# Scores of a gated cross-attention block: one product of 127 rows a head, with the mask among its rows

## What is computed

```python
scores = einsum('bhqd,bhkd->bhqk', qh, kh) / sqrt(16)        # 16 heads of 16; q = layernorm(x), k = v = ctx
causal = triu(ones((256, 77)), k=1)                          # later keys
merged = where(causal == 1, causal, mask[:, None, None, :])  # and padded keys
attn = softmax(where(merged == 1, -inf, scores))
x = x + tanh(g_xattn) * (einsum('bhqk,bhkd->bhqd', attn, vh) @ W.T + b)
x = x + tanh(g_ffn) * ffn(layernorm(x))    # SwiGLU shared expert, two groups of four experts, the best two
```

## Time and profile before

| | us |
|---|---|
| median of 3 runs | 1140.37 |
| lowest and highest | 1137.81, 1147.08 |
| the profiled execution | 1138.31 |
| its span in the trace | 1136.6 |

### The profile page before, as it was taken

The page is one execution under the profiler, slowest core; times in us unless marked ns, Lnnn a source line. Parts: engine busy times, 40 slices in busy tenths (PEclk is TensorE's granted clock), DMA queues, the critical chain, the costliest instruction groups (busy, mean ns, idle before and its releaser), DMA issues.

```text
span 1136.6 us, 22381 instructions
## 1 busy us (share of the span) xinstructions
PE 1084.2 (95%) x7411; PEld 908.4 (80%) x7411; DVE 818.2 (72%) x1810; ACT 472.3 (42%) x722; POOL 520.0 (46%) x644
## 2 busy tenths in 40 slices
PE   5689999999999999999999999999999999999997
PEld 3467888888788787788888777888887888888886
DVE  7757786886876876877878676557544688888886
ACT  4565556555555555655555432233221111111111
POOL 5334447457357456465563534000001566666564
PEclk8989999999999999999999999999999899999999
DMA  8975748666765764766666112687652554555451
GB/s 157 244 159 120 147 102 129 135 126 102 146 137 123 119 146 106 113 141 128 99 128 145 29 55 74 209 260 242 214 173 104 163 157 154 163 166 150 148 175 64
DMA packets 106162, 160.64 MB, mean 141 GB/s; under 512 B 28828, under 2 KB 70718, under 8 KB 106048
## 3 DMA queue, kind: packets, MB, share of 16 engines
q1 hardware_dynamic: 94276, 121.18, 46.8%
q0 software_dynamic: 11776, 38.03, 11.1%
HBM read 75.24 MB, written 52.10 MB: 112 GB/s over the span
## 4 chain that ended last, share of the span: by engine, by line
PE 71%; issue 11%; DVE 7%; POOL 6%; DMA 3%; ACT 2%; SPq 1%; POOLq 0%; DVEq 0%; ACTq 0%
PE ps L764 16%; PE ps L811 12%; PE ps L709 7%; PE ps L726 7%; PE ps L813 6%; PE ps L631 4%; PE ps L796 3%; PE ps L619 3%; PE ps L662 2%; POOL tab_dram L1471 2%; PE ps L585 2%; PE ps L589 2%; POOL x L1447 2%; DMA regr<-regr 2%; PE ps L640 1%
## 5 line engine op out<-in xcount | busy, mean ns | idle before, releaser
L811 PE MATMUL ps<-regr,gh 128*128 x600 | 221.6, 407 | 0.2 <-issue 0.2
L888 ACT ACTIVATE Pt<-ps,pbias 77x1024 f32<-77x1024 f32 x128 | 141.6, 1106 | 98.2 <-PE ps L619 96.8
L813 PE MATMUL ps<-regr,gl 128*128 x600 | 170.0, 283 | 0.0
L811 PEld LDWEIGHTS ps<-regr,gh 128*128 128x128 f32 x600 | 113.8, 190 | 23.9 <-issue 0.6
L978 ACT ACTIVATE gh<-ps 128x512 fp32r<-128x512 f32 x75 | 44.8, 599 | 204.9 <-PE ps L796 204.9
L1189 DVE TENSOR_REDUCE mneg<-ps 128x8 f32<-128x616 f32 x128 | 100.4, 792 | 21.3 <-PE ps L589 21.1
L813 PEld LDWEIGHTS ps<-regr,gl 128*128 128x128 f32 x600 | 114.0, 190 | 0.0
L709 PE MATMUL ps<-x2h,winh 128*128 128x512 f32 x256 | 108.2, 423 | 0.6 <-DVE OHR L1093 0.6
L1379 POOL TENSOR_TENSOR gl<-gf,gh 128x512 fp32r<-128x512 f32 x64 | 82.7, 1293 | 42.8 <-ACT gh L850 42.6
L1447 POOL TENSOR_TENSOR x<-x,regf 128x512 f32<-128x512 f32 x32 | 41.1, 1285 | 132.7 <-DMA x<-in_x 132.7
L709 PE MATMUL ps<-x2h,winl 128*128 128x512 f32 x256 | 100.6, 393 | 0.0
(11 more groups left out here) (201 smaller groups left out, 2652.9 us busy)
## 6 DMA issues: line engine op xcount, KB each, us to landing
regr<-regr SPq DMA_DIRECT2D x96, 256.0 KB, 5.9
y_dram<-Pt SPq DMA_DIRECT2D x64, 256.0 KB, 2.4
regf<-in_x SPq DMA_DIRECT2D x32, 256.0 KB, 4.3
x<-in_x SPq DMA_DIRECT2D x32, 256.0 KB, 7.2
y_dram<-res SPq DMA_DIRECT2D x32, 256.0 KB, 2.4
regr<-regr SPq DMA_DIRECT2D x96, 77.0 KB, 6.9
x_dram<-x2h SPq DMA_DIRECT2D x14, 512.0 KB, 3.0
x_dram<-x2l SPq DMA_DIRECT2D x14, 512.0 KB, 3.8
```

The lines of the kernel that those rows point to most:

```text
L811: e.matmul(o, gh2[:, k % 3, fc, :], w2v[:, bass.ds(val, 1), fc, :, :].rearrange("p o h d -> p (o h) d"), start=fc == 0, stop=False, skip_g ...
L813: m = e.matmul(o[:, 0, :], gl2[:, k % 3, fc, :], w2v[:, bass.ds(val, 1), fc, 0, :].rearrange("p o d -> p (o d)"), start=False, stop=fc == ...
L888: e.activation(Pt[0:K, 4 * k:4 * k + 4, :].rearrange("k (n j) t -> k n (j t)", n=2), bank_of["sc", b, k][0:K, :, :], ACT.Exp, bias=pbias[: ...
```

## The change

1. The mask of later keys becomes part of the score product. `Kst` and `Xs` get 77 rows ahead of the others: `cauT` (now the transposed triangle, -3e38) for all heads in `Kst`, an identity for tokens 0 to 76 and zero behind in `Xs`. Both are written once (`own` on ACT, `diagonal` on DVE). The L614 products go. The rows are 77 (mask) + 3 x 16 (high, low, high of the keys) + 2 (maxima) = 127, still with 77 output rows and 256 columns.
2. The rows of the other head half are no longer zero: `Xs` is kept per half j as well, so each product sees its own 48 rows only. A query copy is cut in two, with 64 source rows into 16 rows: six DMAs of 128 KB for three of 256 KB. `maxT` writes 2 rows instead of 4.
3. The keys are sent for each batch row by itself: stage `spread` in slot 9 of every step, six DMAs with rows of 616 bytes. `Kst` has buffers for two batch rows where it had them for two pairs. `kv` moves from slot 11 of odd steps to slot 2 of the even step behind it, and waits for all key copies before it; `keys` moves to slots 4 and 6.
4. Padded keys are overwritten in `kf` by the first unpadded one (`ramp` falls from 77, and padded keys get 1000 less), which leaves the maximum as it is without a mask: stages `marks`, `table` and `pick` on DVE (three operations for two batch rows, slot 9 of odd steps), with a small table in DRAM from which `load_kv` also loads `pk` for the two rows. `pad`, `first`, the two long mask copies and POOL's L1440 go; of the L589 products those for t = 0 stay, with `caus` alone.

```diff
-    order += [("load_x", 0, 0), ("load_kv", 0, 0), ("load_x", 1, 0), ("consts", 0, 0), ("moments", 0, 0), ("kv", 0, 0),
-              ("masks", 0, 0), ("pads", 0, 0)]
+    order += [("load_x", 0, 0), ("load_masks", 0, 0), ("load_kv", 0, 0), ("load_x", 1, 0), ("consts", 0, 0), ("moments", 0, 0),
+              ("marks", 0, 0), ("pick", 0, 0), ("kv", 0, 0)]
...
-        put(i, ((1, "keys", 0), (3, "keys", 1)))
+        put(i, ((1, "keys", 0), (3, "keys", 1)) if i == 0 else ((4, "keys", 0), (6, "keys", 1)))
+        put(i, ((9, "spread", 0),))
         if i == 0:
+            slots[5].append(("table", 0, 0))
...
+            slots[7].append(("diagonal", 0, 0))
...
         if i % 2 == 1 and i + 1 < NB:
-            slots[11] += [("kv", i // 2 + 1, 0), ("vau", i // 2 + 1, 0)]
+            slots[9].append(("pick", i // 2 + 1, 0))
+            slots[11].append(("vau", i // 2 + 1, 0))
+        if i % 2 == 0 and 0 < i < NB:
+            slots[2].append(("kv", i // 2, 0))
...
+                elif stage_ == "spread":
+                    e.wait_ge(s["klo"], b // G + 1)
                     if b >= 2:
-                        e.wait_ge(s["sc"], 4 * G * (b - 1))
-                    spread_kv(b)
...
+                        e.wait_ge(s["sc"], 4 * (b - 1))
+                    for r, t in enumerate((khi, klo, khi)):
+                        for j in range(2):
+                            o = K + DH * r
+                            dst = Kst[o:o + DH, h, j, :, :, :].rearrange("p q c k -> p (q c k)")
+                            src = t[64 * j:64 * j + 64, b % G * 2:b % G * 2 + 2, :]
+                            e.dma_start(dst.bitcast(F), src.bitcast(F)).then_inc(s[f"kd{h}"], 16)
...
                     for r, t in enumerate((xTh, xTh, xTl)):
-                        dst = Xs[32 * r:32 * r + 32, h, :, :, :].rearrange("p q c t -> p (q c t)")
-                        e.dma_start(dst.bitcast(F), t[:, h, :, :].bitcast(F)).then_inc(s[f"xs{h}"], 16)
+                        for j in range(2):
+                            o = K + DH * r
+                            dst = Xs[o:o + DH, h, j, :, :, :].rearrange("p q c t -> p (q c t)")
+                            e.dma_start(dst.bitcast(F), t[64 * j:64 * j + 64, h, :, :].bitcast(F)).then_inc(s[f"xs{h}"], 16)
...
-                    if k == 0:
-                        e.wait_ge(s["first"], b + 1)
-                    for q in range(2):
-                        m = e.matmul(o[:, q], identb[:, :], (pad[:, b, :] if t else first[:, h, :]).unsqueeze(1).broadcast_to([P, 4, K]),
-                                     start=False, stop=True)
...
+                    if t == 0:
+                        for q in range(2):
+                            m = e.matmul(o[:, q], identb[:, :], caus[:, :].unsqueeze(1).broadcast_to([P, 4, K]), start=False, stop=True)
...
                     for n in range(2):
-                        e.matmul(pair[0:K, n, :].rearrange("k (j t) -> k j t", j=2)[:, :, 0:K], identb[0:K, 0:K],
-                                 cauT[:, :].unsqueeze(1).broadcast_to([K, 2, K]), start=True, stop=False, skip_group_check=True)
-                    for n in range(2):
                         p, bk = 2 * k + n, pair[:, n, :]
                         for j in range(2):
-                            m = e.matmul(bk[0:K, j * S:(j + 1) * S], Kst[:, ks, j, p % 4, 2 * g + p // 4, :],
-                                         Xs[:, h, p % 4, p // 4, :], start=False, stop=j == 1, skip_group_check=True)
+                            m = e.matmul(bk[0:K, j * S:(j + 1) * S], Kst[:, h, j, p % 4, p // 4, :], Xs[:, h, j, p % 4, p // 4, :],
+                                         start=True, stop=True)
...
                 if stage_ == "kv":
-                    e.wait_ge(s[f"kf{h}"], 16 * (b // 2 + 1))
+                    e.wait_ge(s["pick"], 3 * b + 3)
                     if b >= 1:
                         e.wait_ge(s["kbd"], 2 * G * b)
-                        e.wait_ge(s[f"kd{1 - h}"], 96 * ((b - 1) // 2 + 1))
+                        for n in range(2):
+                            e.wait_ge(s[f"kd{n}"], 96 * b)
...
+                elif stage_ == "diagonal":
...
+                    v = Xs[0:K, b, :, :, :, :].rearrange("r j q c t -> r (j q c) t")
+                    e.memset(v[:, :, P:S].bitcast(F), 0.0).then_inc(s["dcon"], 1)
+                    e.tensor_copy(v[:, :, 0:P], ident[0:K, :].unsqueeze(1).broadcast_to([K, H, P])).then_inc(s["dcon"], 1)
...
+                elif stage_ == "pick":
...
+                    e.tensor_tensor(kone[:, :, :, :], v, pk[:, h, :, 1, :].unsqueeze(2).broadcast_to([P, G, 2, K]),
+                                    ALU.mult).then_inc(s["pick"], 1)
+                    e.wait_ge(s["pick"], 3 * b + 1)
+                    e.tensor_reduce(kfirst[:, :, :], kone[:, :, :, :], AX, ALU.add).then_inc(s["pick"], 1)
+                    e.wait_ge(s["pick"], 3 * b + 2)
+                    e.copy_predicated(v, pk[:, h, :, 0, :].bitcast(I32).unsqueeze(2).broadcast_to([P, G, 2, K]),
+                                      kfirst[:, :, :].unsqueeze(3).broadcast_to([P, G, 2, K])).then_inc(s["pick"], 1)
```

More of the change, by code:

```diff
@@ L17 @@
 G = 2
-KR = 100
+KX = K + 3 * DH + 2
 HID = 512
@@ L28 @@
 YD = 3 * D
-REG = 22016
+REG = 23648
 RY = 8
@@ L423, in load_kv @@
                     s[f"vf{h}"], 16)
-            def spread_kv(b):
-                h = b % 2
-                for r, t in enumerate((khi, klo, khi)):
-                    for j in range(2):
-                        o = 32 * r + 16 * j
-                        dst = Kst[o:o + 16, h, j, :, :, :].rearrange("p q a k -> p (q a k)")
-                        e.dma_start(dst.bitcast(F), t[64 * j:64 * j + 64, :, :].bitcast(F)).then_inc(s[f"kd{h}"], 16)
             for stage_, b, k in order:
@@ L1538 @@
         _np.diff([p_[0] for p_ in pairs]), _np.diff([p_[1] for p_ in pairs])]).astype(_np.float32)
-    own = _np.zeros((4, 2, H, K), _np.float32)
-    for r_ in range(4):
-        own[r_, r_ % 2] = 1.0
-    arrays["own"] = own.reshape(4, -1)
     nc = _bacc.Bacc("TRN2", target_bir_lowering=False, num_devices=1)
```

145 lines of the change are left out of this document (80 added, 65 removed), and 4 rows, old and new, of the table names.

## The result

The change makes the kernel slower by 11%: 1268.3 us (median) where the runs of before beside it have 1140.4, a ratio of 1.110 [1.106, 1.114]. The forecast was 1188 us with a range up to 1225, so the sign and the place are as forecast and the size is not: about 49 us were foreseen, 128 came.

A forecast was written before the change was run, and what follows sets the result against it. PE bounds the kernel before; afterwards the path over x (SP, transfers, POOL, DVE) does: +4.2 us a pair, +52 over 12.5 pairs, less some 3, start 0. 1138.3 + 49 = about 1188 us, own range 1165 to 1215, 8 in 10 1115 to 1225.

The forecast's parts named there:

- The place and the chain: Phase one: key copies ahead of x delay its landing, POOL's bias addition, `gl` and DVE, so PE waits; +49 us.
- The issue price: On SP: each copy takes 0.63 us to issue, per copy and not per row; lower bound 0.37.
- Short issues: Rival on SP: half-size copies take 0.37 us instead of 0.63, total about 1150 us; chance 0.14.
- The rows of the product: PE score products growing from 100 to 127 rows: between 0 and 0.01 us each, taken as 0.
- `pick`: DVE's three added operations per two batch rows: 1.5 us in odd steps, in DVE's idle time, taken as 0.
- Slow transfers: Rival on the query copies: writing half the rows takes twice as long, x lands after 14.8 us, about 1340 us; chance 0.06.
- The first rival: PE stays the bound, the burst hidden because x still comes before it is needed: -28 us, 1110; chance 0.24.
- PE's saving: Mask products gone from PE: 1.04 us a step, -28 us over 27 steps if nothing else comes late.
- The new period: Steps from L489 to L489: 22.6 us even to odd, 22.0 odd to even; a pair 44.6 against 40.4.
- Landing: From first query to x landed, bound by transfers: taken as 8.7 us, between 8.1 and 9.3.
- From x to the next L494: From x's landing to the next copy of the maxima (L489 before): 9.3 us even to odd, 8.3 odd to even.
- The start: Kernel start, new DVE work against removed fills and mask copies: taken as 0, between -7 and +11 us.

The follow-up runs named there:

- third filling: Kernel after with 18 products of constants ahead of the values products of even rows, written into the bank these then overwrite: 1268.4 us, ratio 1.110.
- the fillings one and two: Kernel after with constant products in an open shared-expert bank, one piece a slot earlier; the second in even rows alone: 1338.4 and 1322.2 us.

## Why the prediction was wrong

**What held.** The place and the chain: twelve copies in front of x, POOL late, DVE's L1254 (before L1218), then `gl` and the values. Each link is in the rows above, and moving one load undoes it. The issue price was right: 0.63 us a copy, x issued at L494 + 8.4 in most even steps as summed (0.8 + 3.8 + 3.8), 9.0 to 10.5 for 8.8 in odd ones. Short issues were rightly small. The rows of the product cost close to nothing (L619: 307 ns in the mean for 297 in the earlier trace rows, at the lower clock), and so does `pick`.

**Slow transfers** was rightly small: from the first query to x landed it is 10.0 us with 16 rows a copy where it was 9.3 with 32 (the rival had 14.8), and with the queries alone cut in two x lands 9.9 us after the maxima in even steps, where it was 10.0. The Trainium skill, "SBUF — State Buffer", section "Door 1: The DMA port swizzle", lets the rate of a DMA go with the number of ports that its partitions reach, 189 GB/s for 32 partitions and 104 for 16 at 1 MiB; from these figures the query copies would take 1.8 times as long, an estimate. The traces don't agree: 10.0 us for 9.3, and 9.1 to 9.7 in even steps with the queries alone cut in two.

**The first rival**, PE stays the bound, was wrong twice: x can't be 4 us later (it lands 4.6 us later in even steps, and PE waits), and even where x is on time the -28 us are not there. Taking PE's saving as 1.04 us a step is right as work (PE's busy time goes from 494 of 500 us, 20.0 in a step of 20.27, to 476, 19.1 in a step of 20.1, in the version with x first and late key products) and wrong as time: the next bounds, x's path and probably the banks of the maxima, lie within 1 us of PE.

**The step that failed** is "The new period". A pair was put at 44.6 us and is 49.8: two of its terms were too small, and a third, the clock, was missing.

- *Landing.* First query to x landed was taken as 8.7, between 8.1 and 9.3. It is 10.0 (321.66 to 331.63), and from x's issue 6.2 and 6.7 us in the two steps shown where the sum left 4.9. I let the longer issue overlap the transfers and took the lower half of the range; the burst didn't become shorter at all. The DMA engines are as full as in the earlier trace rows:

```profile
328.00:330.00 2.00, 2.00 (x20) 2.00 (x18) 0.80 (x1) 1.22 (x2) 0.00 (x0) 1.00 1.10 113
```

  x lands on average at 14.7 (even) and 15.5 us (odd) for 13.3 and 13.7: 1.4 and 1.8 us of the error, 1.6 a step. The six issues and the 16 rows alone did not make the burst longer: with only the queries cut in two it is 9.1 to 9.7 us in even steps from the first query to the landing, and 9.8 to 10.2 in nearly all of the kernel after. The key copies just ahead are what that run lacks; no run changes their transfers alone.
- *From x to the next L494.* Taken over from before as 9.3 and 8.3; it is 9.9 in most even steps and 8.7 or 10.3 in odd ones, 1.0 us a step too long on average. A part is DVE beside POOL's key products, which I had put into that stretch as free, "which is in the 9.3": with these late it is 8.9 in even steps at the full clock.
- *The clock.* No term had it. The stretches of before show 1.00, and the prediction kept that without a word, while forecasting that PE would wait in every step. Behind many of PE's waits the granted clock falls to its lower level, in the kernel after for 7 to 10 us at a time (columns as in the earlier trace rows):

```profile
350.00:360.00 10.00, 7.07 (x47) 5.78 (x49) 3.72 (x9) 4.90 (x7) 2.43 (x2) 1.00 0.85 149
360.00:370.00 10.00, 6.36 (x42) 3.39 (x35) 7.84 (x21) 2.00 (x4) 5.94 (x10) 0.51 0.02 6
```

  PE was busy 7.1 of the 10 us ahead of the fall. Not every wait brings it: the clock is 1.00 from 430 to 440 us, with a wait of 2.5 us in it. With 2.3 us of length for 3.4 us of lost clock (0.13 of 25.9 us) in the run that filled the waits, the 0.09 that the kernel after loses of 24.9 us would be worth 1.5 us a step. That is an estimate from two kernels. A second one, from the seven steps of the third filling at 0.98 to 1.00: they take 23.5 us in the mean, and the same seven places in the kernel after 24.6, at 0.90, so 1.1 us. Both are more than the 1.0 us a step of the second term, in which most of it has to lie, since the way from L494 to the landing runs over SP and the DMA engines; so they are rather upper bounds, and the clock is not added to that term.

So 22.3 us predicted, about 1.6 for the landing and about 1.0 behind it give the 24.9 measured between 100 and 600 us. What the second consists of is shown at single places (0.9 us of an even step is the late key products, 0.9 us of every fourth step goes with the lower clock), and how it divides in the mean stays open: no run takes the clock's share away alone, and the third filling raised the clock by 0.02 and gave nothing net.

**The start** was taken as 0 within -7 and +11, and is +9.8 at the sixth L494 of the profiled pair; five other runs with this start (the fillings one and two aside) reach it at 113.6 to 114.5 us for 116.1, and two with the start of before at 107.3 and 107.5 for 106.3, which makes some +7. The bound was right and the choice in the middle was not. On DVE, `marks`, `pick` and `table` end at 12.3 us, and the fill and the copy for the first diagonal stand ahead of the second moments:

```profile
16.41 1.76 DVE L1175 MEMSET regr<- 77x2048 f32 x1 [0.37 <-issue]
18.09 1.16 DVE L1176 CAST regr<-ident 77x2048 fp32r<-77x2048 f32 x1
19.17 0.74 DVE L989 BATCH_NORM_STATS2 st<-regf 128x6 f32<-128x256 f32 x2
```

In the kernel before, the moments were there 7.5 us earlier, and the first L489 7.7:

```profile
5.71 2.11 DVE L1147 MEMSET regr<- 96x2464 f32 x1 [0.46 <-issue]
...
11.63 0.74 DVE L986 BATCH_NORM_STATS2 st<-regf 128x6 f32<-128x256 f32 x2
```

Of what was to balance the new work, only this zero fill (2.1 us) and one operation on the masks (0.3) had stood ahead of the moments; the other fill and the long mask copies came later. Moving `table` and the diagonals behind the moments gives 3.4 us of the first L494 back and 3 of the sixth, so what holds the steps between is not settled.

## What to carry to other kernels

Count the DMA instructions that stand on a queue ahead of a load somebody waits for, not their bytes: cutting copies in two or sending them more often was paid here at 0.63 us each by whatever stood behind them. Moving that one load forward may repair a change that looks broken, so the order of the issues belongs to the change. And in a kernel like this one, in which PE and the path over x were within 3% of each other (40.4 and 39.3 us a pair), work taken off PE gave nothing while the other path stayed as it was; where PE began to wait, its clock fell in parts, so put a term for it into a forecast in which PE is to wait.

## What the runs showed of the hardware

- SP takes 0.63 us to issue a copy within SBUF, with 8, 38.5, 128 or 256 KB and 16, 64 or 128 source rows; some bursts of six took 4.0 to 5.1 us in place of 3.75.
- In the kernel after, the granted clock of PE falls from 1.00 to 0.50 (2.4 to 1.2 GHz) for 10 us at 360 and for 7 at 411 us, right behind waits that had left PE idle for 2.5 and 2.0 us; at 430 us it stays at 1.00 behind a wait of 2.5 us. Removing 1 us of PE work a step from a kernel with 99% busy PE brought the mean clock of 100 to 600 us from 1.00 to 0.97 and the time up by 0.7%.
- Small DVE operations took far longer where POOL worked on its key products (128 x 616) beside them: 32 elements a row 550 to 576 ns in the mean for 192 to 229, 256 elements 1441 ns for 417. The busy share of DVE thus depends on when POOL works: 86 of 100 us with the key products in slots 4 and 6, 82 with them in 8 and 10, for the same instructions.
